# Reordering a few waits and transfers in a one-core Macaron block (two mixture-of-experts layers around attention)

## The reference

```
x = x + 0.5 * ffn(layernorm(x))
x = x + attn(layernorm(x))
x = x + 0.5 * ffn(layernorm(x))

ffn(x):  w, idx = top_k(softmax(x @ Wg + bg), 2); w = w / sum(w)
         y_e = relu(x @ W1[e] + b1[e]) @ W2[e] + b2[e];  sum over the two chosen e of w_e * y_e
attn(x): 16 heads of 8 features; c = heads - mean over the 512 tokens
         out = softmax(c @ c^T) @ heads
```

## Time and profile before

| | us |
|---|---|
| median of 3 runs (1015.1 to 1018.54) | 1017.07 |
| the profiled execution's own time | 1015.89 |
| its span in the trace | 1014.1 |

### The profile page before, as it was taken

One profiled execution on the slowest core, in us unless ns is written; L12 is line 12 of the kernel. 1 busy time (PEld: TensorE's weight loads), 2 busy tenths in 40 slices (PEclk: granted clock), 3 DMA queues, 4 the chain that ended last, 5 costly groups with the idle time before them and its releaser, 6 DMA issues.

```text
span 1014.1 us, 20376 instructions
## 1 busy us (share of the span) xinstructions
PE 966.3 (95%) x6528; PEld 538.1 (53%) x6528; DVE 795.0 (78%) x2271; ACT 833.1 (82%) x1194; POOL 525.9 (52%) x623
## 2 busy tenths in 40 slices
PE   7999999999999999998999999999999999999995
PEld 5687777623223288872332323332588883247774
DVE  5899999967776799875778787778788775469997
ACT  4655554499999988888999999999999989976653
POOL 5546777754434504435676667776200005666775
PEclk7999999999999999999999999999999999999999
DMA  6453232000024224530111111161344431243443
GB/s 187 149 176 133 103 105 105 17 17 20 19 82 124 67 96 161 174 123 24 33 35 35 38 38 38 35 193 51 87 138 145 146 112 60 65 136 112 134 157 124
DMA packets 59821, 96.15 MB, mean 95 GB/s; under 512 B 9179, under 2 KB 30403, under 8 KB 59715
## 3 DMA queue, kind: packets, MB, share of 16 engines
q1 hardware_dynamic: 47568, 71.50, 21.8%
q0 software_dynamic: 10752, 22.04, 7.3%
q10 hardware_dynamic: 1396, 1.31, 0.4%
HBM read 56.36 MB, written 38.45 MB: 94 GB/s over the span
## 4 chain that ended last, share of the span: by engine, by line
PE 54%; ACT 19%; issue 11%; DVE 8%; DMA 3%; POOL 2%; SPq 1%; ACTq 0%; POOLq 0%; DVEq 0%
ACT probs L2052 12%; PE ps L1796 9%; ACT sums L2052 6%; PE ps L1781 5%; PE ps L745 3%; PE ps L1400 3%; PE ps L1401 3%; PE ps L1402 3%; PE ps L761 3%; PE ps L1386 2%; DVE low L1020 2%; PE ps L747 2%; PE ps L1412 2%; PE ps L746 2%; PE ps L1416 2%
## 5 line engine op out<-in xcount | busy, mean ns | idle before, releaser
L2052 ACT ACTIVATE probs<-ps 128x1024 f32<-128x1024 f32 x345 | 353.2, 1156 | 11.0 <-PE ps L1781 10.8
L1736 POOL DMA_INDIRECT found<-tiles,home x168 | 166.9, 993 | 190.2 <-ACT probs L2052 140.3
L1724 POOL DMA_INDIRECT sorted<-xn,slot x168 | 167.5, 997 | 176.3 <-ACT probs L2052 60.7
L1796 PE MATMUL ps<-probs,value 128*32 128x512 f32 x1380 | 243.6, 604 | 3.0 <-ACT probs L2052 1.4
L2052 ACT ACTIVATE sums<-ps 128x1024 f32<-128x1024 f32 x167 | 188.6, 1157 | 2.7 <-PE ps L1781 1.8
L1201 ACT ACTIVATE high<-ps 128x512 fp32r<-128x512 f32 x176 | 101.6, 593 | 71.9 <-PE ps L747 69.8
L1781 PE MATMUL ps<-shared 32*128 32x512 f16 x1024 | 147.7, 384 | 10.4 <-ACT probs L2052 2.8
L1796 PE MATMUL ps<-sums,value 128*32 128x512 f32 x668 | 148.7, 604 | 0.2 <-ACT probs L2052 0.2
L1020 DVE SCALAR_TENSOR_TENSOR low<-ps,high 128x512 fp32r<-128x512 f32 x176 | 112.7, 680 | 8.8 <-ACT high L1201 8.6
L1781 PEld LDWEIGHTS ps<-shared 32*128 32x128 f16 x1024 | 39.2, 91 | 148.1 <-ACT probs L2052 69.1
L1277 POOL TENSOR_TENSOR sums<-sums 128x512 f32<-128x512 f32 x59 | 76.3, 1293 | 60.5 <-DVE sums L1052 48.1
(11 more groups left out here) (207 smaller groups left out, 1895.0 us busy)
## 6 DMA issues: line engine op xcount, KB each, us to landing
found<-sorted SPq DMA_DIRECT2D x56, 256.0 KB, 2.7
tiles<-sums SPq DMA_DIRECT2D x56, 256.0 KB
probs<-gates SPq DMA_DIRECT2D x24, 512.0 KB, 5.7
wide<-gates SPq DMA_DIRECT2D x20, 512.0 KB, 6.0
sorted<-zeros SPq DMA_DIRECT2D x16, 512.0 KB
out<-X SPq DMA_DIRECT2D x15, 256.0 KB, 2.4
sorted<-xn,slot POOLq DMA_INDIRECT x168, 2.3
found<-tiles,home POOLq DMA_INDIRECT x168
```

What stands on the lines that cost most here:

```text
L1724: nc.gpsimd.indirect_dma_start(sorted_rows[group_of(q)], bass.IndirectOffsetOnAxis(ap=slot[:, q % XNS, k, j:j + 1], axis=0), xn[:, rows_sl ...
L1736: nc.gpsimd.indirect_dma_start(found[:, q % 2, k, j, :], None, tile_rows[group_of(q)], bass.IndirectOffsetOnAxis(ap=home[:, q, k, j:j + 1] ...
L1796: ins = nc.tensor.matmul(ps[q * W:(q + 1) * W, MIX, :], value[:, s % 2, sd, j, m, q, :], ring[ring_at(g * UNITS + 2 * j + q // 2)][:, q % ...
L2052: nc.scalar.activation(ring[ring_at(n)], ps[:, score_banks(n), :], ACT.Exp, scale=SCORE).then_inc(sm["a_probs"], 1)
```

## The change

Small edits, which fall in seven groups:

- **First job's gates.** PE turns job 0's gates right after expert 0, ahead of the hidden rows of expert 2; ACT copies them ahead of the relu of expert 2; SP issues the first two experts' gates as two transfers of 256 KB with a semaphore each instead of one of 512 KB. Nine matmuls on zeros (`keep_warm`) are put between job 0's logits and their transpose.
- **Start of attention.** DVE's last `scale` of job 6 goes ahead of `route_gates`; on PE the scores of units 2 and 3 go ahead of the first mix.
- **Logits' turn.** `route_turn_logits` moves from unit 3 to unit 6 of `hg` 2, behind `attn_back`; DVE's copy of the result (`r_lg`) moves from inside `attn_high_rows` to behind `attn_shift`; `attn_back` now waits for the flat copy alone, and the next `attn_turn` (`hg` 3) waits for `r_lg`.
- **Means.** In the two `RUSH` sequences `attn_means` moves from unit 4 to unit 6 of `hg` 1.
- **After a stream.** Scores of unit 3 go ahead of the last tile's turn back. The ring's order after a stream is changed so that the buffer of the stored tile is used first by unit 9, not 7; units 6 to 8 reuse a buffer after five units instead of six.
- **Powers.** In sequence 5 the two `norm_pool` go to steps 0 and 1 of POOL's list, from 2 and 4, ahead of collects.
- **Last jobs.** ACT's `ffn_norm_rows_scaled` goes ahead of `scale_half`; the two halves of the second-last collected sequence are scaled and added at experts 5 and 6 of the last job, not 3 and 4.

```diff
-         (2, 3): 16, (2, 4): 17, (2, 7): 18, (3, 0): 19, (3, 3): 20, (3, 4): 21}
+         (2, 3): 16, (2, 4): 17, (2, 7): 18, (3, 0): 19, (3, 5): 20, (3, 6): 21}
...
-            return (0, 1, 5, 2, 3, 4)[(k - RING + 1) % RING]
+            return (0, 1, 2, 3, 5, 4)[(k - RING + 1) % RING]
...
-            return n - (RING - 1 if leg(n) and since_pause(n) == RING - 1 else RING)
+            return n - (RING - 1 if leg(n) and RING - 1 <= since_pause(n) < RING + 3 else RING)
...
-            for e in range(0, E, AHEAD):
-                sp.wait_ge(sm["w1_shifted"], CHUNKS if e else CHUNKS // 2)
+            sp.wait_ge(sm["w1_shifted"], CHUNKS // 2)
+            sp.wait_ge(sm["f_gates_stored"], 16)
+            for e, signal in ((0, sm["f_first_gate"]), (1, gates_ahead[side(0)])):
+                sp.dma_start(gates_on_all[side(0)][:, e:e + 1, :],
+                             gates_dram[side(0):side(0) + 1, e:e + 1, :].to_broadcast([P, 1, T])).then_inc(signal, 16)
+            sp.wait_ge(sm["w1_shifted"], CHUNKS)
+            for e in range(AHEAD, E, AHEAD):
                 spread_part(0, e)
...
                 ffn_logits(pe, 0)
+                keep_warm(pe, 9)
                 ffn_turn_logits(pe, 0)
...
                         ffn_expert(pe, 0)
+                        ffn_turn_gates(pe, 0)
                     if m + 2 < last * E:
                         ffn_hidden(pe, m + 2)
...
-                    if m == 0:
-                        ffn_turn_gates(pe, 0)
...
-                    dve.wait_ge(gates_ahead[u], 16 * uses(n))
+                    if n == 0:
+                        dve.wait_ge(sm["f_first_gate"], 16)
+                    else:
+                        dve.wait_ge(gates_ahead[u], 16 * uses(n))
...
+                if n == 0 and e == 1:
+                    dve.wait_ge(gates_ahead[side(0)], 16)
...
                         if e == 7:
                             route_stats(dve, EARLY)
+                            scale(last * E - 1)
...
-            if last < JOBS:
-                scale(last * E - 1)
-            else:
+            if last == JOBS:
...
+                ffn_copy_gates(act, 0)
                 relu(2)
-                ffn_copy_gates(act, 0)
...
+                    if n < last - 2 and e == 3:
+                        ffn_norm_rows_scaled(act, n + 2)
                     if (n - WHOLE, e) in ADDED:
                         at = ADDED[n - WHOLE, e]
                         scale_half(act, GROUP[1] + at // TOPK, at % TOPK)
                     if n < last - 2:
-                        if e == 3:
-                            ffn_norm_rows_scaled(act, n + 2)
...
                 if i == b:
                     attn_scores(pe, first + 2)
+                    attn_scores(pe, first + 3)
...
                     if n == 0:
+                        attn_scores(pe, 2)
+                        attn_scores(pe, 3)
                         attn_mix(pe, 0, 0)
-                    if n + 2 < b * UNITS and not (g in PAUSES and k == 0):
+                    if n + 2 < b * UNITS and not (g in (0, *PAUSES) and k < 2):
                         attn_scores(pe, n + 2)
...
+                        if hg == 3 and job is not None:
+                            pe.wait_ge(sm["r_lg"], job + 1)
...
-                    if k == 3 and hg == 2 and job is not None:
-                        route_turn_logits(pe, job)
...
                         if hg == 2 and job is not None:
-                            pe.wait_ge(sm["r_lg"], job + 1)
+                            pe.wait_ge(sm["r_flat_copied"], job - EARLY + 1)
...
-                    if k == 4 and hg == 1 and s + 1 < S:
+                    if k == (6 if s in RUSH else 4) and hg == 1 and s + 1 < S:
...
+                    if k == 6 and hg == 2 and job is not None:
+                        reached(pe, sm["a_normed"], g // SIDES)
+                        route_turn_logits(pe, job)
...
-            if job is not None:
-                route_copy_logits(dve, job)
...
                     attn_shift(dve, s + 1)
+                if hg == 2 and job is not None:
+                    route_copy_logits(dve, job)
...
-                if n == PAUSES[y] * UNITS + 7:
+                if n == PAUSES[y] * UNITS + 9:
                     tiles_stored(act, TILE0[y + 1])
...
-                if i == 2 and more:
+                if i == (0 if s == TILED else 2) and more:
                     norm_pool(pool, "a_", s + 1, (s + 1) % 2)
-                if i == 4 and job is not None and late(s):
+                if i == (1 if s == TILED else 4) and job is not None and late(s):
                     norm_pool(pool, "r_", job, route_place(job))
```

More of the change, by code:

```diff
@@ L419, in build @@
  f_rank f_top f_below f_weight f_picked f_total f_inv f_gate f_again
- f_gturned f_gate_rows f_gates_stored f_gates_ahead_even f_gates_ahead_odd f_gates_rest_even f_gates_rest_odd
+ f_first_gate f_gturned f_gate_rows f_gates_stored f_gates_ahead_even f_gates_ahead_odd f_gates_rest_even f_gates_rest_odd
  f_vare a_vare r_vare f_stats f_hidden f_high f_low f_expert f_scaled f_summed f_back f_added
@@ L1896, in build, with attn_high_rows @@
         heads = cent[:, :, :].rearrange("p j d -> p (j d)").rearrange("p (h i) -> p h i", i=HD)
-        def attn_high_rows(dve, s, job):
+        def attn_high_rows(dve, s):
             twice = heads.unsqueeze(2).to_broadcast([P, J * H, 2, HD])
@@ L2006, in attn_vector @@
                 if hg == 2 and more:
-                    attn_high_rows(dve, s + 1, job)
+                    attn_high_rows(dve, s + 1)
                     attn_low_rows(dve, s + 1)
```

## The result

The changed kernel takes 1008.71 us in the median of four executions, the kernel before, run beside it, 1017.27: a ratio of 0.9915 with a 95% interval from 0.9896 to 0.9935. Forecast were 1009.6 us. The profiled execution took 1008.67, its span is 1006.9.

A forecast was written before the change was run, and what follows sets the result against it. Bounds: PE in whole jobs, ACT in attention, DVE and POOL's collects at the end. Terms 1.7 + 1.3 + 2.5 - 0.65 + 0.7 + 1.9 = 7.45 us off gave 1009.6 us, range 1004.5 to 1013.

The forecast's parts named there:

- First job's gates: First whole job: gates turned and broadcast earlier, nine added matmuls; 1.7 us gained, range 0.8 to 2.8.
- Start of attention: Stop of 1.57 us before ACT's third exponential goes, 0.3 given back at the fifth; 1.3 gained, between 0.8 and 1.6.
- Logits' turn: Attention: moving PE's logits' transpose removes ACT's short stops, 2.98 us in all; 2.5 gained, between 0.8 and 3.0.
- Means: Sequences 4 and 13, later sum: 0.8 us lost in 4, 0.15 gained in 13; together -0.65, between -2.2 and +0.4.
- After a stream: Sequence 5: the eighth exponential's 0.68 us wait for the tile's store goes; 0.7 gained, nothing counted after the second stream.
- Powers: Sequence 5: POOL's powers ahead of its collects end ACT's stops of 0.26 and 1.73 us; 1.9 gained, 0.3 at worst.
- Last jobs: Last stretch, bounded by DVE and POOL's collects, neither getting less work: 0, give or take 0.75 us.
- a third of the way down: First job: how the forecast said it took 1.7 us between 2.0 - 0.9 - 0.3 and 2.0 + 0.8.
- if the clock stays low, the logits' transpose is 0.9 late: First job: nine added matmuls take 4.0 us in a 3.08 gap, delaying DVE's ranking and gates by 0.9.
- The added wait: Attention: the next group's turn now needs DVE's logits copy; costed at nothing, 0.1 us a sequence in the lower end.
- so I count a loss of 0.8 there: Sequence 4: PE's later sum makes DVE and its copy of the mixed rows 0.8 us late, up to 1.8.
- last stage that changes by more than 1 us: End of the kernel: one of the signs named as showing the prediction wrong; the last stage was expected as long as before.

## Why the prediction was right, and where not

- **The sum.** 7.45 forecast, 7.2 between the spans. That it came so near is luck: the logits' turn (+1.9), the scores and the ring after a stream (+1.1) and the powers (+0.4) gave more, the means (-1.5), the late store and the last jobs (-2.6 together) less.
- **First job's gates.** 2.0 against 1.7 in the two profiles, and not by the steps given, so this too is luck. The recorded 1.7 is also not "a third of the way down" from 2.8 to 0.8, which is 2.1. Before's execution was a long one: the same code came 2.58 earlier in the kernel with the means alone, where the clock stayed at 1.00 from 30 to 34. Against that one (196.8) the two executions without calls (mean 195.0) gain 1.4 and 2.2, which is what the prediction gave for the reordered gates, 1.9 to 2.0; the seven with the calls (mean 197.9) gain nothing. So the calls, 2.9 us in the mean, take all of it; there are only two executions on each of the two small sides. The step "if the clock stays low, the logits' transpose is 0.9 late" bounded the calls' cost by their length alone. What it missed is that a faster PE frees ACT, ACT frees POOL (18.97 against 19.96 without the calls), and POOL's reads hold DVE's ranking. The forecast's 0.44 us a call was near (4.21 at most for nine), but "at the lower clock level" isn't what the profile's clock says of the twelve that it was read from: 1.00 from 1.38 to 6.68. The rule of the Trainium skill's "TensorE: Matmul & The Clock Gate" (What's actually happening), that activity releases the throttle, is borne out by 1.00 from 14 to 20 (0.50 to 0.74 in the five profiles without them); that the calls then pay for themselves, as the prediction drew from it, is not.
- **Start of attention.** 1.52 against 1.3, and exactly 1.51 in the undoing; the mechanism as told, the fifth exponential's stop included (0.31 for 0.3), makes 1.16 of it, up to the ninth exponential. The other 0.36 was not foreseen: the tenth exponential's stop is 0.21 instead of 0.53.
- **Logits' turn.** The mechanism holds, and only the size was off: 4.4 against 2.5, since a stop costs more than its gap. (The 0.51 of the sum lies in four sequences, not three.) The added wait costs nothing: in the changed kernel PE has no wait before the next group's turn.
- **Means.** -2.15 against -0.65, and the step that failed is PE's clock, which the term leaves out. Where the clock held, the step "so I count a loss of 0.8 there" is right: the late sum costs sequence 4 0.9 to 1.1 us (31.28 to 31.51 against a mean of 30.4), and sequence 13 gives 0.55. The sum was 1.13 late (7.32 after exponential 136 instead of 6.19), and from it to the mix that it delays pass 5.2 us in both kernels, 3.2 of them routing work that stands ahead of the mixed copy in DVE's queue; so ACT stops 1.67. In the changed kernel's profile PE's clock then fell (0.57 from 338 to 342), and the mix, the turn back and the scores behind it in PE's queue took longer: the second stop, of 1.35. Six of the nine executions with the late sum have that fall, none of the five with the early one.
- **After a stream.** The ring is worth 0.73 in the undoing, against 0.7. The scores ahead of the turn back, which the prediction put at nothing, are worth 0.58 after the first stream and 0.45 after the second: the step that failed is that the turn back would lose as much as they win.
- **Powers.** Both stops go: 1.90 for the second and some 0.4 for the first, against 1.9; 2.46 in the undoing.
- **Last jobs.** Given as 0, in the pair -1.63: the "last stage that changes by more than 1 us" that the prediction named as a sign of error is there, with the late store. The new order itself looks ahead by 0.6 to 2.4, in two of three executions more than the 0.75 that was allowed: it takes away a wait of PE behind which the clock fell in those two; with three executions of the old order that is likely, not shown.
- **Open:** why the last store lands 1.8 later in three executions, why the second stream took 1.5 to 1.9 us longer in two, and why the clock falls behind the same wait in some executions and not in others.

## What to carry to other kernels

Before you fill an engine's idle time, or move work two units later, list what it sets free or holds back on the other engines: here nine dummy matmuls in a gap and one sum moved out of a crowd each cost some 2 us or more, both away from where they stood. Price a delay by the in-order queue behind it, not by its length; where it makes PE wait, look at the granted clock behind the wait; and take a stop of a saturated engine from start to start, not from its gap. Where several small edits go in together, time the parts by the starts of a repeated instruction and undo each alone, and look at several executions; the sum can be right with half of its terms wrong.

## What the runs showed of the hardware

- DVE instructions that read two tiles of the state buffer stand still while POOL reads it: `picked` up to 1.30 instead of 0.19, `gate` 0.77 to 1.35 instead of 0.22, the comparison 1.40 instead of 0.42, each ending within 0.3 us of POOL's instruction, and each short again once POOL was held back. `low`, which reads one tile from PSUM and one from the state buffer, keeps its pace beside the same POOL work (two in 1.28). The Trainium skill, "SBUF — State Buffer" (Who interferes with whom), states this: a VectorE instruction with two inputs in the buffer contends with a GpSimd instruction that reads it, the shared ports are an exclusive lock, and issue order decides who blocks. The traces agree: POOL came first by 0.01 us at 18.97 and DVE stood, and POOL came second by 0.07 at 19.96 and DVE did not.
- Nine warm-up calls took 2.79 us where the clock rose early among them (mean 0.72 from 10 to 14) and 4.21 where late (0.52). Without them it rises as well, later: from 14 to 20 its mean is 0.50 to 0.74 in five profiles, and 0.75 to 1.00 in the nine with them.
- PE's granted clock fell to its lower level behind or in a mix that had waited 2.51 us in six of nine executions, and in none of the five where it waited 1.01 to 1.02. At that level the eight matmuls of the changed kernel's next mix lasted 1.76 us (1.07 where the clock held).
- The first 256 KB piece of the broadcast landed 3.05 to 3.36 us after its issue in twelve executions, the first 512 KB piece after 3.83 and 4.29 in two.
- An exponential that is fed in time starts before the one ahead of it ends (0.23 us in the rows of sequence 6 above), so a stop of 0.30 costs 0.40 to 0.53.
